# Space-filling-curve ranks: two blocks made one, Morton keys first, upper triangles compared, column sums on PE

## The reference, cut to what matters

```python
q = _quantize(coords_bn3)
qt = q[..., jnp.array([1, 0, 2])]
keys = [_morton_key(q), _morton_key(qt), _hilbert_key(q), _hilbert_key(qt)]
return [jnp.argsort(kk, axis=1) for kk in keys]
```

## Time and profile before

| | us |
|---|---|
| median of 3 runs | 2311.38 (2309.77 to 2312.67) |
| span of the profiled execution | 2306.2 |
| time of the profiled execution itself | not recorded beside its span |
| DVE busy in the span | 1904.0 (83%) |
| PE busy in the span | 1865.0 (81%) |
| ACT busy in the span | 1616.7 (70%) |
| the two blocks | 0 to about 180 |

### The profile page before, as it was taken

One profiled execution on the slowest core, in us unless ns is written; L12 is line 12 of the kernel. 1 busy time (PEld: TensorE's weight loads), 2 busy tenths in 40 slices (PEclk: granted clock), 3 DMA queues, 4 the chain that ended last, 5 costly groups with the idle time before them and its releaser, 6 DMA issues. The chain is left out here.

```text
span 2306.2 us, 99850 instructions
## 1 busy us (share of the span) xinstructions
PE 1865.0 (81%) x37528; PEld 1286.8 (56%) x37528; DVE 1904.0 (83%) x3658; ACT 1616.7 (70%) x3249; POOL 1007.8 (44%) x995
## 2 busy tenths in 40 slices
PE   0296665888888566499999998677999999999967
PEld 0023335777777344389999997343554544454432
DVE  6798986999999599689989987783888888888865
ACT  0299985888888699689999998456555555555532
POOL 0000006999999200178888886001434444444311
PEclk9997668999999666699999999799999999999979
DMA  2103766666565167655555552212322322222210
GB/s 59 14 1 89 165 163 141 123 122 123 122 123 121 32 157 166 157 110 109 107 105 110 108 105 53 93 28 67 92 83 73 91 74 81 79 85 82 61 56 19
DMA packets 435513, 216.09 MB, mean 94 GB/s; under 512 B 301259, under 2 KB 404843, under 8 KB 435304
## 3 DMA queue, kind: packets, MB, share of 16 engines
q1 hardware_dynamic: 430120, 210.73, 39.2%
q10 hardware_dynamic: 5312, 4.31, 0.8%
HBM read 161.97 MB, written 52.96 MB: 93 GB/s over the span
## 5 line engine op out<-in xcount | busy, mean ns | idle before, releaser
L865 PE MATMUL pQ<-QM,QX 128*128 128x64 f16 (+1 forms) x5760 | 531.5, 216 | 2.1 <-issue 2.1
L863 PE MATMUL pQ<-neigh_lo,QX 128*128 128x32 f16 (+1 forms) x5760 | 519.8, 188 | 2.1 <-issue 2.1
L863 PEld LDWEIGHTS pQ<-neigh_lo,QX 128*128 128x128 f16 x5760 | 494.9, 103 | 5.4 <-issue 2.8
L865 PEld LDWEIGHTS pQ<-QM,QX 128*128 128x128 f16 x5760 | 486.9, 104 | 1.8 <-issue 1.7
L961 POOL TENSOR_TENSOR Dm<-Sc,mx 128x450 f32<-128x450 f32 x384 | 365.8, 953 | 77.8 <-DVE mx L921 77.8
L968 POOL TENSOR_TENSOR Ap<-E,R 128x450 f32<-128x450 f32 x384 | 366.0, 953 | 67.9 <-DVE R L934 57.5
L998 ACT ACTIVATE Vs<-pQ 128x480 f32<-128x480 f32 (+1 forms) x384 | 295.6, 770 | 4.7 <-PE pH L891 3.0
L930 DVE STREAM_TRANSPOSE AT<-Ap 128x480 f32<-128x480 f32 x384 | 259.3, 675 | 33.4 <-PE pH L891 10.9
L1963 POOL TENSOR_TENSOR MT<-cb,decay 128x512 f32 (+1 forms) x128 | 164.0, 1302 | 247.4 <-PEq L1731 150.6
L1011 ACT ACTIVATE E<-Dm 128x450 f32<-128x450 f32 x384 | 224.1, 584 | 60.1 <-POOL Dm L961 60.0
L921 DVE TENSOR_REDUCE mx<-Sc 128x15 f32<-128x450 f32 x384 | 224.0, 583 | 15.2 <-ACT Sc L992 15.1
(11 more groups left out here) (362 smaller groups left out, 3584.5 us busy)
## 6 DMA issues: line engine op xcount, KB each, us to landing
QM<-scratch_q SPq DMA_DIRECT2D x192, 240.0 KB, 2.7
QX<-scratch_q SPq DMA_DIRECT2D x768, 60.0 KB, 2.5
scratch_q<-QT SPq DMA_DIRECT2D x120, 360.0 KB, 4.8
Wg<-in_in_proj SPq DMA_DIRECT2D x64, 256.0 KB, 2.7
Wh<-in_in_proj SPq DMA_DIRECT2D x64, 256.0 KB, 2.8
Wo<-in_out_proj SPq DMA_DIRECT2D x64, 256.0 KB, 2.6
W_s<-in_in_proj SPq DMA_DIRECT2D x16, 256.0 KB, 2.7
CT<-scratch_c SPq DMA_DIRECT2D x192, 11.2 KB, 2.2
```

What stands on the lines that cost most here:

```text
L863: nc.tensor.matmul(pQ[:, p, u // PB, o + 32:o + BW], qx[u], W["neigh_lo"][:, 0:O], start=False, stop=True, skip_group_check=True)
L865: last = nc.tensor.matmul(pQ[:, p, u // PB, o:o + BW], qx[u], qm[u], start=False, stop=True, skip_group_check=True)
```

## The change

The two blocks become one, `keys_and_ranks`.

- DVE makes the pieces of the two Morton sets directly after the coordinates are back (`pieces(0)`), then the Hilbert transformation, then `pieces(1)`. The normalisation of the latents goes behind that, before the folding of the weights.
- The keys are stored and loaded in two parts, with a semaphore each. SP loads Morton set 0 and both Hilbert sets, ACT loads Morton set 1. The constant rows are loaded by ACT after the coordinates are back. SP's loads of `rep`, `place` and `ident` go behind the Morton loads, its store of the latents behind the Hilbert loads.
- For a tile t only the columns from 128 t on are compared. What a point of a later tile has below the diagonal is got from the transposed side: PE multiplies the stored signs (or `less`) with a column of ones, which sums each column over the tile's 128 points, into `sums`.
- In the Morton loop ACT takes both sets; in the Hilbert loop ACT takes set 2 and DVE set 3. The differences of two sets use 2 banks per tile, 4 banks in all.
- After the loops ten small operations of DVE put ranks together.

The core of the diff:

```diff
+        PAIRS = [(t, t2) for t in range(NT) for t2 in range(t + 1, NT)]
+        STEPS = B * NT
-        pw = ctx.enter_context(nc.psum_tensor("pw", [128, 2, 4, 512], F32))
+        pw = ctx.enter_context(nc.psum_tensor("pw", [128, 2, 512], F32))
+        diff = ctx.enter_context(nc.psum_tensor("diff", [128, 2, 2, 512], F32))
+        sums = ctx.enter_context(nc.psum_tensor("sums", [128, 512], F32))
...
+            sp.wait_ge(idx_in, 64)
+            sp.wait_ge(keys_ready, 3)
+            store_keys(0)
+            sp.wait_ge(keys_stored[0], 16)
+            load_keys(sp, 0)
+            for name in ("rep", "place"):
+                sp.dma_start(fixed[name][:, :], io[name]).then_inc(fixed_in, 16)
+            sp.dma_start(fixed["ident"][:, :], io["ident"][0:32, 0:32]).then_inc(fixed_in, 16)
+            sp.wait_ge(keys_ready, 6)
+            store_keys(1)
+            sp.wait_ge(keys_stored[1], 16)
+            for m in (2, 3):
+                load_keys(sp, m)
             sp.wait_ge(latn_ready, 1)
...
+            def differences(curve, b, t):
+                for half in range(2):
+                    for e in range(2):
+                        m = 2 * curve + e
+                        last = nc.tensor.matmul(diff[:, t % 2, e, t * 128:N],
+                                                st_key[32 * m:32 * m + 4, half, b, t * 128:t * 128 + 128],
+                                                mv_key[32 * m:32 * m + 4, half, b, t * 128:N],
+                                                start=half == 0, stop=half == 1)
+                        if half == 1:
+                            last.then_inc((morton_diff, hilbert_diff)[curve], 1)
+            def column_sums(curve, b, t):
+                for e in range(2):
+                    rows = less[:, t, :] if curve and e else sign[:, t, e, :]
+                    for t2 in range(t + 1, NT):
+                        at = ((2 * curve + e) * B + b) * len(PAIRS) + PAIRS.index((t, t2))
+                        last = nc.tensor.matmul(sums[:, at:at + 1], rows[:, t2 * 128:t2 * 128 + 128], ones[:, :],
+                                                start=True, stop=True)
+                last.then_inc(summed, 1)
...
+            for s in range(STEPS + 1):
+                if s < STEPS:
+                    if s >= 2:
+                        pe.wait_ge(signed, 2 * s - 2)
+                    differences(0, s // NT, s % NT)
+                if s >= 1 and (s - 1) % NT < NT - 1:
+                    pe.wait_ge(signed, 2 * s)
+                    column_sums(0, (s - 1) // NT, (s - 1) % NT)
+            pe.wait_ge(keys_in[1], 16 * 12)
+            for s in range(STEPS + 1):
+                if s < STEPS:
+                    pe.wait_ge(signed, 2 * STEPS + s - 1 if s >= 2 else 2 * STEPS)
+                    if s >= 2:
+                        pe.wait_ge(counted, s - 1)
+                    differences(1, s // NT, s % NT)
+                if s >= 1 and (s - 1) % NT < NT - 1:
+                    pe.wait_ge(signed, 2 * STEPS + s)
+                    pe.wait_ge(counted, s)
+                    column_sums(1, (s - 1) // NT, (s - 1) % NT)
...
             act.wait_ge(var_ready, 1)
             nc.scalar.activation(sd[:, :], mv[:, :, 1], ACT.Sqrt).then_inc(sd_ready, 1)
+            act.wait_ge(q_in, 16)
+            for m in range(M):
+                load_units(act, m)
+            act.wait_ge(keys_stored[0], 16)
+            load_keys(act, 1)
+            with act.Fori(0, B) as b:
+                for t in range(NT):
+                    for m in range(2):
+                        act.wait_ge(morton_diff, b * (2 * NT) + (2 * t + m + 1))
+                        if t < NT - 1:
+                            act.wait_ge(summed, b * (NT - 1) + (t + 1))
+                        nc.scalar.activation(sign[:, t, m, t * 128:N], diff[:, t % 2, m, t * 128:N], ACT.Sign,
+                                             accum_out=tally[:, m, bass.ds(b, 1), t]).then_inc(signed, 1)
+            with act.Fori(0, B) as b:
+                for t in range(NT):
+                    act.wait_ge(hilbert_diff, b * (2 * NT) + (2 * t + 1))
...
+            with dve.Fori(0, B) as b:
+                for t in range(NT):
+                    dve.wait_ge(hilbert_diff, b * (2 * NT) + (2 * t + 2))
+                    if t < NT - 1:
+                        dve.wait_ge(summed, b * (NT - 1) + (B * (NT - 1) + t + 1))
+                    v.tensor_scalar(less[:, t, t * 128:N], diff[:, t % 2, 1, t * 128:N], 0.0, 0.0, ALU.is_lt,
+                                    ALU.add, accum_out=rank[:, bass.ds(b + 3 * B, 1), t]).then_inc(counted, 1)
...
+            part = sums[:, 0:M * B * len(PAIRS)].rearrange("p (x k) -> p x k", k=len(PAIRS))
+            link(v.memset(below[:, :, 0], 0.0))
+            link(v.tensor_copy(below[:, :, 1:3], part[:, :, 0:2]))
+            link(v.tensor_tensor(below[:, :, 2], below[:, :, 2], part[:, :, 3], ALU.add))
+            link(v.tensor_reduce(below[:, :, 3], part[:, :, 2:6:2], X, ALU.add))
+            link(v.tensor_tensor(below[:, :, 3], below[:, :, 3], part[:, :, 5], ALU.add))
+            turns = tally[:, :, :, :].rearrange("p m b t -> p (m b) t")
+            link(v.tensor_tensor(turns, turns, below[:, 0:3 * B, :], ALU.subtract))
+            link(v.tensor_scalar(rank[:, 0:3 * B, :], turns, -0.5, (N - 1) / 2.0, ALU.mult, ALU.add))
+            for t in range(1, NT):
+                last = rank[:, 3 * B:, t]
+                link(v.scalar_tensor_tensor(last, last, 128.0 * t, below[:, 3 * B:, t], ALU.add, ALU.subtract))
```

More of the change, by code:

```diff
@@ L136, in norm_and_keys @@
         inv = sb("inv", [128, 2])
-        pw = ctx.enter_context(nc.psum_tensor("pw", [128, 2, 4, 512], F32))
+        sign = sb("sign", [128, NT, 2, N], F16)
+        less = sb("less", [128, NT, N], F16)
+        tally = sb("tally", [128, 3, B, NT])
+        below = sb("below", [128, M * B, NT])
+        ones = sb("ones_r", [128, 1], F16)
+        pw = ctx.enter_context(nc.psum_tensor("pw", [128, 2, 512], F32))
+        diff = ctx.enter_context(nc.psum_tensor("diff", [128, 2, 2, 512], F32))
+        sums = ctx.enter_context(nc.psum_tensor("sums", [128, 512], F32))
         lat_in = sem("lat_in")
@@ L155, in norm_and_keys @@
         turned = sem("w_turned")
+        ones_ready = sem("ones_ready")
+        morton_diff = sem("morton_diff")
+        hilbert_diff = sem("hilbert_diff")
+        signed = sem("signed")
+        counted = sem("counted")
+        summed = sem("summed_r")
         v_chain = sem("v_chain_keys")
@@ L194, in _ @@
         def _(pe):
+            pe.sem_inc(summed, NT - 1)
             pe.wait_ge(w_in, 16 * 7)
@@ L203, in _ @@
+                nc.tensor.matmul(pw[:, l, C + 128:C + 129], convT[:, l, :], blin[:, l:l + 1], start=True, stop=True)\
                     .then_inc(folded, 1)
-            for l, W in enumerate(weights):
-                O = W["O"]
-                pe.wait_ge(scaled, l + 1)
-                for side in range(2):
-                    last = nc.tensor.transpose(pw[:, l, 2 + side, 0:O],
-                                               eff[0:O, l, side, :, :].rearrange("p c m -> p (c m)"), ident[0:O, 0:O])
-                last.then_inc(turned, 1)
+            def differences(curve, b, t):
[8 more added lines that the diff above has]
+                            last.then_inc((morton_diff, hilbert_diff)[curve], 1)
@@ new lines, in _ @@
+            for s in range(STEPS + 1):
[8 more added lines that the diff above has]
+                    column_sums(1, (s - 1) // NT, (s - 1) % NT)
+                if s == 1:
+                    for l, W in enumerate(weights):
+                        O = W["O"]
+                        pe.wait_ge(scaled, l + 1)
+                        for side in range(2):
+                            last = nc.tensor.transpose(pw[:, l, side * O:(side + 1) * O],
+                                                       eff[0:O, l, side, :, :].rearrange("p c m -> p (c m)"),
+                                                       ident[0:O, 0:O])
+                        last.then_inc(turned, 1)
@@ L218, in _ @@
             act.dma_start(ident[:, :], io["ident"]).then_inc(w_in, 16)
-            for m in range(M):
-                for tile, side, at in ((mv_key, 0, 32 * m + 2), (st_key, 1, 32 * m)):
-                    act.dma_start(tile[at:at + 2, :, :, 0:N].rearrange("r h b n -> r (h b) n"), io["units"][side])\
-                        .then_inc(keys_in, 16)
             act.wait_ge(var_ready, 1)
             nc.scalar.activation(sd[:, :], mv[:, :, 1], ACT.Sqrt).then_inc(sd_ready, 1)
-            act.wait_ge(keys_stored, 16)
-            for m in (2, 3):
-                load_keys(act, m)
+            act.wait_ge(q_in, 16)
[15 more added lines that the diff above has]
+                    if t < NT - 1:
+                        act.wait_ge(summed, b * (NT - 1) + (B * (NT - 1) + t + 1))
```

(20 more changed lines are left out.)

159 lines of the change are left out of this document (51 added, 108 removed).

## The result

The changed kernel takes 2322.27 us (median of 4 runs, 2321.48 to 2323.41), the kernel before 2310.57 us (4 runs, 2306.80 to 2312.67). The ratio is 1.0044, with a 95% interval of 1.0025 to 1.0062: slower by about 12 us. Forecast were 2330 us and slower.

What follows compares the result with a forecast made beforehand. Latency before 99.6 us, then DVE's compares, were taken to bound the edited part; the new loops, PE-ACT round trips. 47.0 + 79.6 + 67.8 + 4.7 = 199.1 us against 180.2, hence 2306.2 + 18.9 + 5.2 = 2330 us, range 2309 to 2345.

Steps and rivals of the forecast that it cites:

- Part 1: Front of the block: first compare at 47 us, between 37 and 54, which is 52.6 us earlier than before.
- a hold of one packet in all: Morton key store: by the skill, held at most one constant-row packet, about 2.7 us; the forecast kept 7.8 us.
- the few partitions set the rate: Morton key loads: destination partitions set the rate, so 13.1 us to the first matmul despite half the loads.
- Part 2: Morton loop: a chain of signs, column sums and differences gives 4.97 us a batch, 79.6 us for 16.
- Part 3: Hilbert loop: the chain gives 4.24 us a batch, 67.8 us in all; making and loading its keys is hidden.
- Part 4: End of the block: weight splits, small operations and block change put the next block 4.7 us after the last count.
- The sum: Whole edited block: next block at 199.1 us where the trace has 180.2, 19 us later.
- The 5.2: Microseconds around the span: runs' median 2311.4 us against the profiled span of 2306.2, added to the forecast.
- (a): Rival, both loops: engines set the pace, Morton 52.5 us, Hilbert 16 x 1.68; kernel 2262 us; chance 6%.
- (b): Rival, both loops: PE at 2.4 GHz saves 0.64 us per batch and loop, 20.5 in all; 2310 us; chance 10%.
- (c): Rival, column sums: weight loads paid in full, 28 us more in both loops, 2358 us; chance 12%.
- (d): Rival, front: key loads early, first compare at 37 us, chain as priced, 2320 us; chance 15%.

Runs made afterwards that it cites:

- Experiment 4: The kernel before with PE's starting credits halved, so it runs two pairs of key sets ahead instead of four: 2371.67 us, ratio 1.0267.
- 1: The changed kernel with each step's column sums issued after the differences two steps later: 2309.78 us, ratio 0.9995 to the kernel before.
- 9: The changed kernel with three PSUM banks per set turned by step number, later column sums, ACT and DVE loops written out: 2291.04 us, ratio 0.9911.
- 5: The changed kernel with the eight constant-row loads back at the head of ACT's queue: 2321.69 us, ratio 1.0056 to the kernel before.
- 6: The changed kernel with constant rows written by four GpSimd memsets instead of loaded: 2318.35 us, ratio 1.0042 to the kernel before.
- 10: The kernel of 9 with constant rows written by four ACT copies instead of loaded: 2281.13 us, ratio 0.9858 to the kernel before.
- 7: The changed kernel with fifty dense matmuls, results unused, run on PE before the Morton loop: 2320.68 us, ratio 1.0051 to the kernel before.

## Why the prediction was right

**Direction and mechanism.** Right: the first compare came 50 us earlier, each step then waited for a round trip that four slots had hidden, and both loops together cost more than was won. Experiment 4 shows the round trip in the kernel before, and 1 and 9 give its parts in the changed one: with the same elements and the same slow matmuls the block ends 196.1 - 159.2 = 36.9 us earlier, 13.1 of them by the place of the sums and 23.8 by the ring of three and the written-out loops together.

**Part 1, first compare at 47.0; measured 49.8.** Three errors, of both signs. Keys ready at 23.8, not 26.0: store and load of the coordinates took 2.0 and at most 2.2 us, not 3.2 and 3.0. The loads of the keys took 12.3 us (13.1 said). The store of the keys took 13.7 us, outside the bounds of 3.2 and 9.8. The failed step was to carry over the duration of the coordinates' store. In both stores seven eighths of the packets go at once, and the rest stands still for 5.1 to 5.2 us beside the constant rows. But this rest was 6 packets of 2048 bytes for the coordinates (18.5 to 18.9 us in the kernel before), moved in 0.4 us, and 128 of 128 bytes for the keys, moved in 5.5 us, one for each packet of the constant rows. Experiments 5, 6 and 10 show the same store in 2.2 to 2.3 us when the constant rows are over or absent. The Trainium skill ("DMA: Bandwidth & Descriptors", "Queues, rings and completion order") says that an engine goes round the queues that have work, one packet of each. The prediction read this as a hold of one packet in all. By packets of this trace it is one for each packet of the store's own, as the 129 packets beside 130 from 30.4 to 36.1 us show. The 5.1 us of standstill before them it does not explain; their cause stays open.

That eight loads of keys would take about as long as sixteen came true (12.3 us, 13.1 before), but its reason, that the few partitions set the rate, is not shown. The change also put the loads of `rep`, `place` and `ident` (164 KB) right behind them on SP's queue. From 44.4 to 49.6 us only SP's queue moved anything to speak of, 0.14 MB, which is the size of `place`, and the keys' last completions came at 49.7. All runs on the changed kernel have this order, so none tells whether those loads delay the first compare.

**Part 2, batch 4.97 us; measured 4.67.** Mis-sized terms: from engine to PE 0.05 us, not 0.12 (twice); the column sums 0.25 and 0.15 us, not 0.39 and 0.23. Differences and start of ACT were right (0.81 and 1.25 us, said 0.81 and 1.23). The loop took 75.1 us, 4.5 less than forecast. One sign that the prediction named failed: ACT was busy 30.75 of 40 us, 77%, and not at most two thirds.

**Part 3, batch 4.24 us; measured 4.02**, for the same two reasons: 2.4 us less. That the Hilbert keys are hidden held: their loads were issued at 74.8 to 79.2 us, the loop began at 124.9.

**Part 4, 4.7 us; measured 5.8.** The exchange of blocks took 1.64 us of waiting, not 0.8, and the operations 0.3 us more.

**The sum.** 2.8 - 4.5 - 2.4 + 1.1 = -3.0: the block at 196.1, not 199.1. That it came so close is partly luck: the store of the keys alone was 5.9 us too short in the forecast, and errors the other way hid it. The profiled execution was forecast at 2330.3 us and took 2323.4, 6.9 less: 3.0 by the block, 0.5 by the rest, and 3.4 because 2323.4 - 2321.6 = 1.8 us lie around its span and not 5.2. The 5.2 mixed what lies around a span with the difference between one execution and the median of others.

**The rivals.** (a) engines set the pace: false here. In 9 it came true, in the Morton loop at the price named (16 x 3.34 = 53.4 us, said 52.5); the Hilbert loop took 3.06 us a batch and not the 1.68 named, since the price left out PE. (b) 2.4 GHz: false; its price was right, since the one batch of 7 at 2.4 GHz saved 0.60 us (0.64 said), but neither dense work ahead nor within held the clock. (c) weight loads paid in full: false, six sums took 0.25 us. (d) loads early: false, they were late.

## What to carry to other kernels

A saving of work is worth little in a loop held by round trips: count the steps between an engine's result and its next input, divide by the depth of the ring, and compare with the busy time of the slowest engine, PE's passes at the clock of that loop among them, before cutting elements. A ring has the depth of its most shared slot, and in-order queues spread that wait to all steps behind it, so turn the slots by step. A small transfer that shares some DMA engines with a slow one is as late as its rows on those engines, which here went one for one with the slow one's after a standstill: count rows, not bytes. Where the content of the slow transfer is constant, an idle engine can write it.

## What the hardware did that I had not expected

- A store of 128 KB took 13.7 us beside loads that used 0.14 of the DMA engines, and 2.2 us without them. Seven eighths of it were moved within 1.7 us of its issue; the last eighth took the rest. The Trainium skill, "DMA: Bandwidth & Descriptors", "Why a DMA increments its semaphore by 16 and not by 1", says that a transfer is spread over as many engines, up to 16, as divide its slowest dimension. For the constant rows that is 2; 2 of 16 is 0.125, near the 0.14 and equal to the eighth of the store that was late.
- One DVE operation took 7.12 us instead of 0.54 beside GpSimd's memsets; beside ACT's writes of the same bytes it did not.
- ACT and GpSimd fill 128 x 4112 float32 in about the same time, 3.57 and 3.50 us (7.15 and 6.99 for two).
- Eight loads of key rows take 12.2 to 12.7 us from issue to the first compare in the changed kernel and seven runs on it, always with `rep`, `place` and `ident` behind them; before there were 16 in 13.1.
